# Eight turns instead of four in each pass of the engines' loop, in a kernel for attention and a gated feed-forward

## What is computed

```python
xn = _layernorm(x)
q, k, v = (xn @ w + b for each of 16 heads, 8 wide)
scores = softmax(q @ k.T / sqrt(8))
att = concat(scores @ v) @ wo.T + bo
xr = mu_r * xn + (1 - mu_r) * xn_prev
xk = mu_k * xn + (1 - mu_k) * xn_prev
ffn = sigmoid(xr @ W_r.T) * (square(relu(xk @ W_k.T)) @ W_v.T)
return x + att + ffn
```

## Time and profile before

| | us |
|---|---|
| median of three runs | 468.74 |
| lowest, highest | 467.95, 469.03 |
| the profiled execution | 469.65 |
| its span in the trace | 467.5 |

### The profile page before, as it was taken

The page is one execution under the profiler, slowest core; times in us unless marked ns, Lnnn a source line. Parts: engine busy times, 40 slices in busy tenths (PEclk is TensorE's granted clock), DMA queues, the critical chain, the costliest instruction groups (busy, mean ns, idle before and its releaser), DMA issues.

```text
span 467.5 us, 16068 instructions
## 1 busy us (share of the span) xinstructions
PE 446.1 (95%) x5384; PEld 268.7 (57%) x5384; DVE 400.8 (86%) x825; ACT 386.0 (83%) x868; POOL 367.0 (79%) x674
## 2 busy tenths in 40 slices
PE   6688999999999999999999999999999999999996
PEld 5334565656555665556665666656565656666554
DVE  7578899989988999899998899899998999989831
ACT  2138889888888899988998999989988989899893
POOL 6668788878877888888888888888888888887321
PEclk8559999999999999999999999999999999999999
DMA  4543455544455454344554544455444544554200
GB/s 128 156 124 96 126 160 145 145 128 125 121 149 150 134 158 125 110 140 137 159 157 127 148 132 118 126 148 159 145 139 129 146 118 130 148 150 135 62 15 24
DMA packets 86061, 60.43 MB, mean 129 GB/s; under 512 B 6224, under 2 KB 73808, under 8 KB 86032
## 3 DMA queue, kind: packets, MB, share of 16 engines
q1 hardware_dynamic: 86032, 60.06, 44.8%
HBM read 29.89 MB, written 29.36 MB: 127 GB/s over the span
## 4 chain that ended last, share of the span: by engine, by line
PE 87%; issue 3%; DMA 3%; ACT 2%; DVE 2%; SPq 1%; ACTq 0%; DVEq 0%; POOL 0%
PE bank_val L653 26%; PE bank_exp L733 19%; PE bank_max L743 10%; PE misc L762 4%; PE misc L794 4%; PE misc L668 4%; PE misc L689 3%; PE misc L773 3%; PE misc L843 3%; PE misc L833 3%; PE misc L697 2%; PE misc L801 2%; ACT probs L460 1%; DMA ops<-spill 1%; DVE neg_max L570 1%
## 5 line engine op out<-in xcount | busy, mean ns | idle before, releaser
L570 DVE TENSOR_REDUCE neg_max<-bank_max 128x2 f32<-128x512 f32 x512 | 327.9, 685 | 39.2 <-PE bank_max L743 34.1
L460 ACT ACTIVATE probs<-bank_exp 128x512 f32<-128x512 f32 x504 | 273.6, 597 | 30.3 <-PE bank_exp L733 28.2
L733 PE MATMUL bank_exp<-ops 51*128 51x256 bf16 x1008 | 157.9, 272 | 8.1 <-issue 6.1
L743 PE MATMUL bank_max<-ops 48*128 48x256 bf16 x1024 | 164.0, 277 | 0.0
L653 PE MATMUL bank_val<-probs,val 128*25 128x256 f32 x2048 | 136.3, 384 | 0.9 <-ACT probs L460 0.8
L733 PEld LDWEIGHTS bank_exp<-ops 51*128 51x128 bf16 x1008 | 73.1, 95 | 72.2 <-issue 49.5
L653 PEld LDWEIGHTS bank_val<-probs,val 128*25 128x25 f32 x2048 | 50.3, 103 | 51.7 <-issue 26.3
L743 PEld LDWEIGHTS bank_max<-ops 48*128 48x128 bf16 x1024 | 74.0, 96 | 4.0
L362 POOL TENSOR_SCALAR xn<-x_in,moments,rstd 128x128 f32<-128x128 f32 x62 | 49.2, 800 | 0.0
L401 POOL TENSOR_TENSOR mixed_x<-mixed_x,xn_t 128x512 f32<-128x512 f32 x32 | 40.7, 1271 | 2.5
L488 ACT COPY xn_t<-misc 128x512 f32<-128x512 f32 (+1 forms) x36 | 19.7, 546 | 24.3 <-PE misc L801 13.5
(11 more groups left out here) (79 smaller groups left out, 615.5 us busy)
## 6 DMA issues: line engine op xcount, KB each, us to landing
ops<-spill SPq DMA_DIRECT2D x126, 192.0 KB, 3.4
spill<-qk_h SPq DMA_DIRECT2D x64, 192.0 KB, 3.4
spill<-qk_m SPq DMA_DIRECT2D x64, 128.0 KB, 2.0
x_in<-x SPq DMA_DIRECT2D x32, 128.0 KB, 2.2
spill<-qk_l SPq DMA_DIRECT2D x32, 128.0 KB, 1.9
y_out<-y SPq DMA_DIRECT2D x32, 128.0 KB, 1.9
ops<-shift SPq DMA_DIRECT2D x128, 6.0 KB
w<-weights SPq DMA_DIRECT2D x1, 448.0 KB, 3.1
```

The lines of the kernel that those rows point to most:

```text
L460: nc.scalar.activation(probs[g % 2][:, u % G, :, :], exp_bank(u, live)[:, :, :], ACT.Exp, scale=SCALE).then_inc(exp_done[u], 1)
L570: nc.vector.tensor_reduce(out=neg_max[hf][:, :, r, pr], in_=bank_max[MAX_BANK[v]][:, :, :], axis=AX_X, op=ALU.max, negate=True).then_inc(m ...
L733: exp_mm = nc.tensor.matmul(exp_bank(u, live)[:, i, :], ops[p][rows, hf, 1, pr, i * P:(i + 1) * P], ops[p][rows, hf, 0, pr, :], start=True ...
L743: max_mm = nc.tensor.matmul(bank_max[MAX_BANK[v]][:, i, :], of[rows, max_hf, 0, max_pr, i * P:(i + 1) * P], of[rows, max_hf, 1, max_pr, :] ...
```

## The change

The body of the loop holds eight turns and is passed three times, for the same turns 4 to 27. `TURN`, which is also the number of buffers of x and of their semaphores, stays at four. The turns before and after the loop are written out as they were.

```diff
 TURN = 4
-LOOP = (1, 7)
+PASS = 2 * TURN
+LOOP = (1, 4)
...
-            for t in range(T_FIRST, TURN * LOOP[0]):
+            first = TURN - PASS
+            for t in range(T_FIRST, first + PASS * LOOP[0]):
                 straight(t)
             with eng.Fori(*LOOP) as k:
 
-                done = {j: eng.compute_val(k * TURN + (j + 1)) for j in range(-3, TURN + 5)}
-                transferred = {(j, m): eng.compute_val(k * (16 * m * TURN) + 16 * m * (j + 1))
-                               for m in transfers for j in range(-1, TURN + 2)}
-                pair = {j: eng.compute_val(k * (8 * TURN) + 16 * (j + 1)) for j in range(-2, TURN // 2 + 2)}
-                quad = {j: eng.compute_val(k * 16 + 16 * (j + 1)) for j in range(0, 3)}
-                for c in range(TURN):
-                    step(k * TURN + c, c, lambda d, c=c: done[c + d], lambda d, m, c=c: transferred[c + d, m],
+                done = {j: eng.compute_val(k * PASS + (first + j + 1)) for j in range(-3, PASS + 5)}
+                transferred = {(j, m): eng.compute_val(k * (16 * m * PASS) + 16 * m * (first + j + 1))
+                               for m in transfers for j in range(-1, PASS + 2)}
+                pair = {j: eng.compute_val(k * (8 * PASS) + (8 * first + 16 * (j + 1))) for j in range(-2, PASS // 2 + 2)}
+                quad = {j: eng.compute_val(k * (4 * PASS) + (4 * first + 16 * (j + 1))) for j in range(0, PASS // TURN + 2)}
+                for c in range(PASS):
+                    step(k * PASS + (first + c), c % TURN, lambda d, c=c: done[c + d], lambda d, m, c=c: transferred[c + d, m],
                          lambda d, c=c: pair[(c + d) // 2], lambda d, c=c: quad[(c + d) // TURN], lambda d: True)
-            for t in range(TURN * LOOP[1], T_LAST + 1):
+            for t in range(first + PASS * LOOP[1], T_LAST + 1):
                 straight(t)
```

## The result

The changed kernel takes 484.22 us (median of 6 runs, 483.0 to 487.16), the kernel before 468.49 us (median of 6). The ratio is 1.034, with a 95% interval of 1.032 to 1.037: 3.4% slower. The forecast was 478.0 us in a range of 470 to 486. The profiled execution took 483.69 us, its span is 481.9 us, against 469.65 and 467.5 before.

The account below looks back on a forecast made before the run. TensorE, busy 95% of the span, sets 13.22 us a turn. Seams +4.7 and fetching +4.5 make +9.2 on the profiled 469.65, 478.9; the median lies 0.9 lower: forecast 478.0 us, range 470 to 486.

Parts of the forecast that it names:

- the rival in which both engines pay more: Code not kept; 2 us for ScalarE's second piece per seam, 8 to 10 us for disturbed transfers: 486, chance 15%.
- Inside a pass TensorE sets the pace; what can change lies at the seams and in the fetching: Turns inside passes take 13.22 us with TensorE always busy; only the excess at seams and in the first pass can change.
- Three seams go, 2.0 us: Three of five backward branches vanish, at 0.67 us each: 2.0 us saved, between 1.5 and 2.6.
- Longer tops, 0.4 us: Extra register instructions at the two remaining seams, on SyncE, ScalarE and TensorE: up to 0.2 us each, 0.4 in all.
- TensorE's twelve pieces are not kept: TensorE's doubled body, eleven or twelve 16 KB pieces, is fetched again every pass; judged four chances in five.
- A missing piece costs TensorE 3.3 us net: At each remaining backward branch TensorE waits for a code piece: 3.5 us, of which its queue covers 0.2 at most.
- The remainder of a seam, 0.70 us: Behind each remaining branch: 0.45 us for VectorE's lateness plus 0.25 for ScalarE's next piece.
- Fetching beside the work, 4.5 us: In turns 8 to 27, 30 TensorE pieces, a fifth meeting the writes of q and k, cost 0.75 us each: 4.5 us.

Follow-up runs that it names:

- e9: Kernel before, with TensorE keeping its loop of four turns and the other four engines' turns written out without a loop: 464.63 us against 468.16, ratio 0.992.
- e4: Bodies of eight turns for VectorE, GpSimd and SyncE only, TensorE and ScalarE at four: 466.97 us against 469.01 for the kernel before, ratio 0.996.
- e3: e2 plus 20 instructions of long-fulfilled waits ahead of ScalarE's loop, moving its head to a piece's beginning: 468.69 us against 469.01 for the kernel before.
- e5: Changed kernel with the loop's backward branch announced by a hint: 484.51 us against 468.44 for the kernel before, ratio 1.035.
- e1: Body of eight turns for TensorE alone, the other four engines at four: 485.91 us against 469.01 for the kernel before, ratio 1.035.
- e7: e1 plus 128 fulfilled waits, 64 instructions, at the start of TensorE's program: 497.88 us against 468.44 for the kernel before, ratio 1.062.
- e12: Kernel before plus a 16 KB scratch transfer in turns 0 to 29, issued by SyncE ahead of the write of qk_l: 476.95 us against 469.33, ratio 1.015.
- e2: Body of eight turns for ScalarE alone, the other engines at four: 478.21 us against 469.01 for the kernel before, ratio 1.020.

## Why the prediction was right, and where it was not

The direction, the mechanism and the range held: 484.2 lies in 470 to 486, but 6 us above the point, near the upper end. It is nearer to the rival in which both engines pay more (486, given 15%) than to the forecast. That rival's 9 us for disturbed transfers were nearer the 7.5 measured than my 4.5. Its 2.45 us behind each gap were as far above the 1.57 measured as my 0.70 were below, and laid to ScalarE where it was the clock; so that its total comes so near is in part luck. Step by step:

- *Inside a pass TensorE sets the pace; what can change lies at the seams and in the fetching.* Right: turns 8, 17 and 18 are at 13.22 us, and e9 shows a loop with no excess at all.
- *Three seams go, 2.0 us.* Right: e4 has this part and gains 2.0 us, longer tops of SyncE included. That TensorE's own branch costs nothing while its code is kept was right as well (e9).
- *Longer tops, 0.4 us.* Not resolved. Turns 12 and 20 of e4, with a longer top on SyncE, took 14.09 and 13.85 us, before 13.96 and 14.10.
- *TensorE's twelve pieces are not kept.* Right, 49 pieces against 17. The Trainium skill's 128 KB for TensorE and 32 KB for the others (page "Advanced Engine Details and Errata", section "ISA Cache") fit the runs: eleven to twelve pieces of 16 KB are not kept, and four of 8 KB are but five are not. Its "Only 2 cache lines!" differs from the trace as before, by the six pieces that TensorE keeps; e3 doesn't settle it for ScalarE, since 338 instructions would fit into two lines of 256.
- *A missing piece costs TensorE 3.3 us net.* Right in size: the first scores come 3.71 and 3.18 us late. With the 1.57 us behind them, a seam's turn is 18.5 and 18.0 us long from one projection to the next, where I had looked for 16.5 to 18. That the gap is a missing piece is shown by e5, which makes it go; how its 3.3 us are made up was not measured.
- *The remainder of a seam, 0.70 us.* The step that failed in size, and partly in kind: it was 1.57 us each time. I had put 0.25 us on a second piece for ScalarE and 0.45 on VectorE. e1 has no missing piece on ScalarE and loses more, and the windows show the cause: the idle time of 3.64 us is followed by about 3.4 us at the lower clock level, and TensorE is busy for the whole turn. VectorE's lateness, which I had carried over, is not seen there either. The sum had no term for the clock. With it the seams are 10.0 instead of 8.0 us.
- *Fetching beside the work, 4.5 us.* The mechanism was right and the term too small: 7.5 us in turns 8 to 27. The guess had one harmful stretch with a fifth of a turn; there are two (5.2 to 6.6 and 0.2 to 1.3 us, nine of twenty turns lose time), at 0.8 us each, which was about the price I took. That it is the fetches was only argued then; the shift in e7 and the landings beside the table now show it. How a fetch holds a write up is open (e12).

These last two terms account for 2.0 + 3.0 of the 5.2 us by which the spans' difference of 14.4 us missed the sum of 9.2.

## What to carry to other kernels

The length of a loop's body is part of its cost. Before it is made longer, count each engine's records in it (here a float32 matmul is four) and look whether the queues that carry code are silent after the first pass; once they were not, every pass here paid at its branch, and fetches that met transfers without slack cost 0.8 us each. Where engines have programs of their own, set the length for each: here the short programs gained from having no loop at all (-0.8%), while the long one had to keep its body of four turns. And when an idle time of TensorE is priced, look for the slower clock behind it: here 1.57 us on a gap of 3.64.

## What the runs showed of the hardware that was not expected

Twenty instructions that do nothing, ahead of a loop, turned 478.2 into 468.7 us, since they moved a body of 338 instructions from five pieces of code to four (e2, e3). In the other direction 64 instructions ahead of TensorE's loop made the gap at a branch grow from 3.35 to 5.03 us (e7). An announced branch removed the gap of 3.6 us at the branch, and behind the loop TensorE and then ScalarE stood still instead, so that 6.3 us were saved inside the loop and 6.0 lost behind it (e5). A fetch of 16 KB, whose own packet takes about 1.1 us, went along with the landing of a write 1.7 us later (3.5 against 1.8), in one turn as in the median of 26.
